# Random-feature attention block on one core: both halves of a group's attention product in succession, and the next batch's projection and split steps reordered

## The reference

```
feature_map(x) = (exp(x @ orf.T / 32**0.25 - |x|^2 / (2*sqrt(32))) + 1e-6) / sqrt(128)
q = feature_map(split(x @ Wq.T + bq)); k = feature_map(split(x @ Wk.T + bk)); v = split(x @ Wv.T + bv)
kv = einsum('nlm,nld->nmd', k, v); ksum = sum(k, over tokens)
out = (q @ kv) / (q @ ksum)
x = layernorm(x + merge(out) @ Wo.T + bo)
x = layernorm(x + x @ ternary(weight).T * scale)
```

## Time and profile before

| what | value |
|---|---|
| median of 3 runs | 1286.36 us (1285.94 to 1286.54) |
| the profiled execution: its time, its span in the trace | 1285.8 us, 1284.0 us |
| PE busy | 1258.4 us, 98% of the span, 8626 matmul records |
| DVE busy | 898.3 us, 70% |
| ACT busy | 713.5 us, 56% |
| POOL busy | 363.5 us, 28% |
| granted TensorE clock, mean | 0.999 |
| load of one x tile on SP's queue, median from issue to landing | 3.1 us |

### The profile page before, as it was taken

How to read it: one execution, slowest core, us unless ns; L and a number is a source line. 1 busy time by engine, 2 the same in 40 slices (tenths; PEclk the granted TensorE clock), 3 DMA queues, 4 the chain that set the end, 5 groups by cost and what they waited for, 6 DMA issues and landing times.

```text
span 1284.0 us, 24908 instructions
## 1 busy us (share of the span) xinstructions
PE 1258.4 (98%) x8626; PEld 957.5 (75%) x8626; DVE 898.3 (70%) x1615; ACT 713.5 (56%) x1435; POOL 363.5 (28%) x745
## 2 busy tenths in 40 slices
PE   9999999999999999999999999999999999999986
PEld 8767787777877678776787768876788767886665
DVE  6588765786668775787657786577765777656766
ACT  5657536574356743667337663367544665356634
POOL 0113332124311333213422134311352123421143
PEclk9999999999999999999999999999999999999999
DMA  7658314772146821566215762267602675036611
GB/s 239 152 132 224 91 45 118 185 188 75 58 124 166 201 60 53 139 177 174 62 58 135 196 152 70 62 146 199 164 31 71 161 202 143 34 92 150 160 39 66
DMA packets 82748, 160.32 MB, mean 125 GB/s; under 512 B 17856, under 2 KB 36416, under 8 KB 82112
## 3 DMA queue, kind: packets, MB, share of 16 engines
q1 hardware_dynamic: 68880, 139.78, 43.5%
q10 hardware_dynamic: 9648, 16.85, 3.5%
q0 software_dynamic: 4096, 2.11, 0.7%
HBM read 39.13 MB, written 16.78 MB: 44 GB/s over the span
## 4 chain that ended last, share of the span: by engine, by line
PE 86%; ACT 5%; issue 2%; DVE 2%; POOL 0%; ACTq 0%; POOLq 0%; DVEq 0%
PE ps L952 25%; PE ps L915 21%; PE ps L965 9%; PE ps L1015 8%; PE ps L983 5%; PE ps L970 4%; PE ps L938 4%; PE ps L940 4%; PE ps L939 4%; PE ps L1041 2%; ACT features L675 2%; ACT squares L658 1%; ACT x_hi L643 1%; PE ps L992 1%; DVE stats L773 0%
## 5 line engine op out<-in xcount | busy, mean ns | idle before, releaser
L675 ACT ACTIVATE features<-ps 128x512 f32<-128x512 f32 x512 | 278.4, 603 | 176.6 <-PE ps L965 128.4
L825 DVE SCALAR_TENSOR_TENSOR unit_lo<-ps,cols,unit_hi 128x512 fp32r<-128x512 f32 x128 | 95.2, 743 | 116.7 <-ACT squares L658 116.7
L965 PEld LDWEIGHTS ps<-orf_stack,stacks 98*128 98x128 f32 x1024 | 130.8, 191 | 27.9 <-issue 20.3
L915 PE MATMUL ps<-Wo_hi,stacks 128*128 128x512 f32 x448 | 150.4, 402 | 0.0
L648 ACT ACTIVATE values_then_attention<-ps 128x512 f32<-128x512 f32 x64 | 38.3, 599 | 194.8 <-PE ps L940 191.6
L567 POOL CAST norm_rows<-norms_turned 128x32 fp32r<-128x32 f32 x64 | 16.5, 257 | 443.4 <-DVE norms_turned L843 443.4
L789 DVE TENSOR_TENSOR den<-den,features 128x512 f32<-128x512 f32 x186 | 127.9, 688 | 10.8 <-ACT features L675 0.5
L965 PE MATMUL ps<-orf_stack,stacks 98*128 98x128 f32 x1024 | 130.4, 272 | 0.0
L551 POOL TENSOR_SCALAR stats<-stats 128x1 f32<-128x1 f32 x128 | 36.3, 283 | 330.5 <-DVE stats L776 330.3
L1015 PE MATMUL ps<-features,kv_ksum 128*32 128x512 f32 x1024 | 123.1, 598 | 4.7 <-ACT features L675 2.2
L656 ACT ACTIVATE unit_hi<-ps,cols 128x512 fp32r<-128x512 f32 x128 | 88.4, 690 | 65.6 <-PE ps L952 65.6
(11 more groups left out here) (132 smaller groups left out, 2596.7 us busy)
## 6 DMA issues: line engine op xcount, KB each, us to landing
stacks<-unit_hi SPq DMA_DIRECT2D x512, 128.0 KB, 2.4
stacks<-unit_lo SPq DMA_DIRECT2D x256, 128.0 KB, 2.7
out<-rows ACTq DMA_DIRECT2D x56, 256.0 KB, 2.0
rows<-in_x_t SPq DMA_DIRECT2D x49, 256.0 KB, 3.1
rows<-in_x SPq DMA_DIRECT2D x32, 256.0 KB, 4.2
features<-in_x SPq DMA_DIRECT2D x32, 256.0 KB, 3.9
values_then_attention<-in_x_t SPq DMA_DIRECT2D x8, 256.0 KB, 6.7
stacks<-norm_rows POOLq DMA_DIRECT2D x128, 16.0 KB, 2.7
```

Source lines behind the costliest of these rows:

```text
L675: nc.scalar.activation(FE[:, n % 8, :, 0:M], ps[:, :].rearrange("p (a m) -> p a m", a=HG), ACT.Exp, scale=C_EXP).then_inc(a_exp.sem, 1)
L825: nc.vector.scalar_tensor_tensor(out=EL[:, u % 2, half], in0=ps[:, :], scalar=BC[:, u:u + 1], in1=EH[:, u % 2, half].bitcast(F32), op0=ALU ...
L915: last = mm(out, a, b, start=(n == 0), stop=(n == len(terms) - 1))
L965: last = mm(ps[:, M * h:M * (h + 1)], slot[0:QK, L * h + P * r:L * h + P * (r + 1)], ORF[0:QK, h, :], start=True, stop=True)
```

## The change

Half 1 of `GG` gets a bank from the ring (2, 3, 4) for its denominators and no longer waits for half 0's. In query units 1 and 3 the `P` part moves ahead of `GG` half 0, so that the halves follow each other, and `Q` half 1 moves behind both. In unit 5 (batches 0 to 6) `S` and `L` half 0 and `XT` 0 move to the front, `F` 6 and 7 and the next batch's `P` part go ahead of both halves of `GG`, and `R` half 0 moves behind `N`. In unit 7 `S` and `L` move ahead of the `F` stages that follow, and `Q` half 0 ahead of `F` 4 and 5.

```diff
     if u < NU - 1:
-        seq = p[0] + (s0 + l0 if u < NU - 3 else []) + f(0, 1)
+        splits = xt(0) if u == NU - 3 else []
+        seq = p[0] + (s0 + l0 if b + 1 < B or u < NU - 3 else []) + splits + f(0, 1)
...
         elif u < NU - 3:
-            seq += kv + f(2, 3) + p[1] + [("KVT", b, g)] + q0 + f(4, 5) + p[2] + s1 + l1 + f(6, 7) + [("GG", b, g, 0)]
-            seq += p[3] + q1 + [("GG", b, g, 1)] + norm + lift + [("R", b, g, 0)]
+            seq += kv + f(2, 3) + p[1] + [("KVT", b, g)] + q0 + f(4, 5) + p[2] + s1 + l1 + f(6, 7)
+            seq += p[3] + [("GG", b, g, 0), ("GG", b, g, 1)] + q1 + norm + lift + [("R", b, g, 0)]
         else:
-            seq += xt(0) + kv + f(2, 3) + p[1] + [("KVT", b, g)] + s0 + l0 + xt(1, 2) + f(4, 5) + xt(3)
-            seq += [("LX", b + 1, t) for t in range(5, TT)] + p[2] + [("GG", b, g, 0), ("R", b, g, 0)] + q0
-            seq += s1 + xt(4) + f(6, 7) + xt(5) + l1 + p[3] + xt(6, 7) + [("GG", b, g, 1)] + q1 + norm + lift
+            seq += kv + f(2, 3) + p[1] + q0 + xt(1) + [("KVT", b, g)] + xt(2) + f(4, 5) + xt(3)
+            seq += [("LX", b + 1, t) for t in range(5, TT)] + p[2] + s1 + l1
+            seq += f(6, 7) + xt(4) + p[3] + xt(5) + [("GG", b, g, 0), ("GG", b, g, 1)] + xt(6, 7) + q1 + norm + lift + [("R", b, g, 0)]
             seq += [("LR", b, t) for t in range(4)]
...
-    seq = p[0] + f(0, 1) + kv + f(2, 3) + p[1] + [("KVT", b, g)] + s0 + l0 + f(4, 5) + [("GG", b, g, 0)] + q0 + [("R", b, g, 0, 0)]
-    seq += p[2] + f(6, 7) + s1 + l1 + [("A", b, 0), ("A", b, 1)] + v0 + [("R", b, g, 0, 1), ("GG", b, g, 1)]
+    seq = p[0] + s0 + l0 + f(0, 1) + kv + f(2, 3) + p[1] + [("KVT", b, g)] + q0 + f(4, 5) + [("GG", b, g, 0), ("R", b, g, 0, 0)]
+    seq += p[2] + s1 + l1 + f(6, 7) + [("A", b, 0), ("A", b, 1)] + v0 + [("R", b, g, 0, 1), ("GG", b, g, 1)]
...
+    if stage[0] == "GG":
+        return (2, 3, 4) if stage[3] else None
     return RING.get(stage[0])
...
+            if kind == "GG":
+                return v_dt, v_dt.nth(b, 2 * k + 2)
...
-                    nc.vector.transpose(turned[:, :, 0:DH], DN[:, :].rearrange("p (a c) -> p a c", c=DH)).then_inc(v_dt.sem, 1)
+                    dens = ps if h else DN
+                    nc.vector.transpose(turned[:, :, 0:DH], dens[:, :].rearrange("p (a c) -> p a c", c=DH)).then_inc(v_dt.sem, 1)
...
                     if half == 0:
 
                         pe.wait_ge(a_kv.sem, a_kv.nth(b, g + 1))
+                        pe.wait_ge(v_dt.sem, v_dt.nth(b, 2 * g))
...
-                    pe.wait_ge(v_dt.sem, v_dt.nth(b, 2 * g + half))
                     pe.wait_ge(a_exp.sem, a_exp.nth(b, 16 * g + 8 + 4 * half + 4))
-                    for bank, c in ((DN, P), (ND[half], 0)):
+                    for bank, c in ((ps if half else DN, P), (ND[half], 0)):
```

## The result

The kernel is slower. Its median is 1296.59 us over four runs (1296.3 to 1299.42), that of the kernel before 1286.45 over four runs beside it (1285.94 to 1287.94): a ratio of 1.0081 (95% interval 1.0066 to 1.0096), and 10.1 us between the medians. The forecast was 1293.0 in a range to 1299. The profiled execution is the slowest of the four, 1299.42 with a span of 1297.6; that of before had a span of 1284.0. Lines behind the edit have moved: L992 is now L998, L1015 is L1021, L965 is L971, L970 is L976, L952 is L958, L789 is L794, L818 is L823.

A forecast was written before the change was run, and what follows sets the result against it. TensorE's own order was taken to set the time. Terms -4.8 + 7.8 + 2.9 + 1.8 - 1.05 gave +6.65 us on the profiled 1285.8, so 1292.4, stated as 1293.0 against the median; range 1286 to 1299.

The forecast's parts named there:

- Pairs: Units 1 and 3: adjacent `GG` halves save 0.30 us in each of 16 pairs, -4.8 in all.
- The waits on the sum: Units 3, 5, 7: `Q` behind half 1 delays DVE's last addition; TensorE waits 0.39 at L992 in 20 places, +7.8.
- Rival 5: Key unit's DVE work slower still: 0.37 more at all 20 waits, 1300 us; chance 0.06.
- Batch 0: Units 3 and 5 of batch 0: no slack left, so the whole 1.46 us appears twice, +2.9.
- Unit 5: Next batch's first `P` part waits for x tile 3, uncovered by `GG` half 0; reorder costs 0.25 a batch, +1.8.
- Last batch: Halves already adjacent there; half 1's own bank ends its wait for DVE's transpose, -1.05 us, once.
- The ring is one use fuller: Half 1's bank is asked for again by `F` 2, after its transpose has ended; cost 0.
- Rival 1: DVE's lateness stays inside the slack because the additions catch up: -4.1, 1282.3 us; chance 0.12.

The follow-up runs named there:

- the faster kernel: The whole change with `Q` half 1 early, but unit 5's `GG` half 0 back ahead of `F` 6 and 7, `R` half 0 following: 1275.23 us, ratio 0.9918.
- the last kernel: Against the faster kernel, last batch's unit 5 has `KVT` ahead of `S` half 1, `Q` and `N` behind both `GG` halves: 1278.51 us, ratio 0.9936.

## Why the prediction was right, and where its sum was not

- **Pairs.** Predicted 0.30 each, measured 0.33 to 0.35. Half to half is 1.74 in each of the 24 pairs, against the 1.76 that two rounds gave, and half 1 takes 1.83. The cost lies where `GG` meets other matmuls, and the second `GG` of a pair doesn't pay it. With that the trace agrees with the Trainium skill (TensorEngine Tiling (Array Packing), Key Properties), which has a change of the tiling mode drain TensorE; no run here tells a drain from another cost of that border.
- **The waits on the sum.** The step was right in place, number and mechanism, and the kernel with `Q` alone moved shows it by itself. The size was 0.39 each, 7.8 in all; measured 9.3. In 16 places it is 0.37 to 0.42. In four it is 0.72 to 0.77, because DVE came some 0.35 later there. Rival 5 had that lateness for all 20 places. By the ends of the additions the trace of before has it in four of 13 places (the prediction says 5 of 15): unit 3 of batches 3, 5 and 7 and unit 5 of batch 2. After the change it is in four of 20: three of these (not batch 3) and unit 7 of batch 1.
- **Batch 0.** Predicted 1.46 twice. Measured 1.46 twice, but 0.92 of it stands at L998 and 0.54 ahead of it, at a `P` part that waits for a late `L`.
- **Unit 5.** The wait for x tile 3 was forecast at 1.6 and is 1.33; the reorder costs 0.06 a batch (0.09 with `Q` early) instead of 0.25. That the halves side by side gain nothing where one of them had covered a wait was right, and the faster kernel prices it: 1282.89 against 1275.23 from that order, with `R` half 0 on DVE, 7.7 us. By blocks it is 1.31 in unit 5 less 0.31 in unit 6, 1.0 in each of seven batches and 7.0 in all.
- **Last batch.** The bank gave 1.09 of the 1.05 forecast. Taken together the batch was mis-forecast: I costed only what its own lines change, but the late DVE of unit 3 also reaches its unit 5, where a `P` part stands ahead of `G` and waits for `L` (+0.99). I had left that place out of the count for having no wait at L992. And the prediction put "The ring is one use fuller" at 0. That failed in unit 6, where the third `F` is given half 1's bank and waits for its transpose, which stands behind `Q` and `N` in this batch, as before the change (+0.95).
- **Key units.** Together 0.8, from `P` parts of 1.45 instead of 1.43. It was not forecast, and it is there without any wait on the sum. It doesn't come with TensorE's new order either: a key unit takes 10.58 or 10.64 in the kernel before too (10.64 in units 2 and 4 of batch 0), and with `Q` alone moved unit 4 takes 10.64 in five batches. Its cause was not found.
- **The clock.** Not forecast: about 2 us in three runs, 5 in the profiled one. By itself it takes the time from 1294.5 or so to where it is.

The mechanism was right, and the number is in part luck. Against the sum of 6.65 the blocks give 8.4, with errors of both signs: pairs -0.6, waits +1.5, unit 5 -1.4, the last batch's two waits +1.95, key units +0.8, blocks behind the waits -0.5. The clock comes on top.

Rival 1, the faster one, gave 1282.3 for the change with DVE's lateness gone. That was measured as 1282.89, with `Q` moved ahead. So the terms of the sum other than the waits were about right together, though not one by one, and the waits on the sum decide the sign.

## What to carry to other kernels

Before an edit to the bound engine's order, read what the edit moves on the other queues. TensorE's gain here was 5.4 us, and a transpose and a reduction put into VectorE's one stretch without idle time cost 9.4 by themselves; the stretch to look for is the one that ends in what the bound engine waits for, however idle the engine is on average. Two halves of work side by side save what their borders with other work cost, but a half that covers a wait is worth more where it is: 0.34 us a pair against 1.0.

## What the runs showed of the hardware

In six of the ten profiled executions of changed kernels TensorE's granted clock fell to 0.50 (1.2 GHz instead of 2.4) in the last batch's unit 5 or 6: for 13.7 us in the kernel after and 10.2 in the last kernel, where it cost 5.2 and about 3.7, and for 3.4 us in four others (units 1 and 3 with `Q` early, units 5 and 7 alone, the bank alone, the last batch as before), where it cost 1.7. Six of them also have 3.4 us at 0.50 in the output stages of that batch, between 1258 and 1282, the fastest kernel among them. Each of the six falls in unit 5 or 6 begins behind a wait for `kv_ksum`, of 1.6 us in five of them and 0.5 in the last kernel. But `Q` alone moved, units 1 and 3 alone, the whole change with `Q` early, the faster kernel and the kernel before have a wait of 1.6 too, and no fall near it.

It is not a matter of one kernel: of the kernel before, three of 14 runs in the first set took 1288.3 to 1289.7, the others at most 1287.4, and the slowest, at 1289.7, had a mean clock of 0.996; in the second set two of 21 took 1289.3 and 1289.5. All four runs of the change have a clock of 0.998 or less, but of `Q` alone moved, with the same waits on the sum in units 3 and 5, four of five have 0.999. The Trainium skill (TensorE: Matmul & The Clock Gate, Part 1: The HAM clock gate) says that the clock follows how busy TensorE has been recently. The two stretches with 7.64 and 7.65 us of work, one followed by a fall and one not, show that the busy time of such a stretch does not decide it here. What does stays open.
